# Attention and coupling network on one core: the third rotation and the last norm, state by state or token by token

## What is computed

```python
x = x + layernorm(attention(layernorm(x)))      # 16 heads of 8 features, softmax over 1024 keys
x = x + layernorm(coupling(layernorm(x)))

def coupling(x):                                # _twist([a, b, c, d]) = [c, -d, -a, b], quarters of 64
    gf = global_net(x.mean over tokens)         # one number per sequence
    out = x
    for _ in range(3):
        tf = coupling_net(out)                  # four layers 256-256-128-64-1, one number per token
        k = 0.1 + ar * (0.7 * gf + 0.3 * tf - 0.5) * 2
        out = out + k * _twist(out)
    return out
```

## Time and profile before

| what | us |
|---|---|
| median of 3 runs | 3399.24 (3398.83 to 3399.82) |
| profiled execution: own span | 3391.6 |
| attention stage of a sequence in the middle | 129 |
| coupling stage of a sequence in the middle | 74 |
| from the last exponential to the end | 129 |

### The profile page before, as it was taken

How to read it: one execution, slowest core, us unless ns; L and a number is a source line. 1 busy time by engine, 2 the same in 40 slices (tenths; PEclk the granted TensorE clock), 3 DMA queues, 4 the chain that set the end, 5 groups by cost and what they waited for, 6 DMA issues and landing times.

```text
span 3391.6 us, 56526 instructions
## 1 busy us (share of the span) xinstructions
PE 3222.9 (95%) x19712; PEld 941.5 (28%) x19712; DVE 2992.7 (88%) x5577; ACT 2843.6 (84%) x3752; POOL 897.6 (26%) x1322
## 2 busy tenths in 40 slices
PE   6989999999999999999999999999999999999987
PEld 2222232322323232232322323232232322323223
DVE  7999989999898998989989898998989989898943
ACT  3868979798897979979798897979979798896975
POOL 5002050321505123050320505123050320504015
PEclk7998999999999999999999999999999999999999
DMA  3111111121111112121121111112121121111001
GB/s 90 26 41 43 32 50 33 44 50 44 50 31 51 43 39 55 33 61 32 44 49 44 50 31 51 42 39 55 33 61 32 45 49 44 38 32 51 8 22 38
DMA packets 97498, 144.75 MB, mean 43 GB/s; under 512 B 49472, under 2 KB 60096, under 8 KB 89408
## 3 DMA queue, kind: packets, MB, share of 16 engines
q1 hardware_dynamic: 93520, 123.83, 13.8%
q0 software_dynamic: 3696, 17.31, 2.8%
HBM read 34.61 MB, written 32.51 MB: 20 GB/s over the span
## 4 chain that ended last, share of the span: by engine, by line
PE 67%; DVE 17%; ACT 8%; issue 3%; SPq 2%; DMA 1%; POOL 1%; DVEq 0%; POOLq 0%; ACTq 0%
PE heads_ps L514 24%; PE ring_ps L481 15%; DVE max_parts L966 12%; PE scoresT_ps L499 11%; PE scoresT_ps L602 7%; ACT p_sb L719 4%; DVE stats L977 3%; PE scoresT_ps L607 2%; ACT headsT L728 1%; PE ring_ps L543 1%; SPq L346 1%; DVE state L1030 1%; ACT state L784 1%; DVE moments L987 1%; PE ring_ps L529 1%
## 5 line engine op out<-in xcount | busy, mean ns | idle before, releaser
L966 DVE TENSOR_REDUCE max_parts<-ring_ps 128x1 f32<-128x512 f32 x3744 | 2369.2, 683 | 225.4 <-PE ring_ps L481 166.3
L719 ACT ACTIVATE p_sb<-scoresT_ps 128x1024 f32<-128x1024 f32 x2048 | 1970.1, 1024 | 81.4 <-PE scoresT_ps L499 57.7
L481 PE MATMUL ring_ps<-k_rows,q_rows 48*128 48x512 bf16 x3744 | 1086.0, 384 | 33.1 <-DVE max_parts L966 23.8
L514 PE MATMUL heads_ps<-p_sb,v_sb 128*9 128x512 f32 x8192 | 1071.4, 595 | 17.9 <-ACT headsT L728 11.9
L499 PE MATMUL scoresT_ps<-q_rows,k_rows 51*128 51x512 bf16 x4096 | 1021.3, 383 | 7.1 <-ACT p_sb L719 4.3
L481 PEld LDWEIGHTS ring_ps<-k_rows,q_rows 48*128 48x128 bf16 x3744 | 265.5, 94 | 1353.4 <-DVE max_parts L966 1242.4
L1233 POOL CAST max_wide<-max_all 128x16 bf16<-128x16 f32 x128 | 25.4, 198 | 1743.0 <-DVE max_all L972 1743.0
L602 PE MATMUL scoresT_ps<-state,w 128*128 128x512 f32 x732 | 364.9, 621 | 13.3 <-DVE state L1030 12.3
L824 ACT ACTIVATE p_sb<-scoresT_ps,b 128x512 f32<-128x512 f32 x180 | 123.8, 688 | 194.2 <-PE scoresT_ps L602 193.2
L499 PEld LDWEIGHTS scoresT_ps<-q_rows,k_rows 51*128 51x128 bf16 x4096 | 207.0, 93 | 224.4 <-ACT p_sb L719 211.5
L514 PEld LDWEIGHTS heads_ps<-p_sb,v_sb 128*9 128x9 f32 x8192 | 124.4, 88 | 288.8 <-issue 278.3
(11 more groups left out here) (196 smaller groups left out, 2635.9 us busy)
## 6 DMA issues: line engine op xcount, KB each, us to landing
q_rows<-parts SPq DMA_DIRECT2D x744, 32.0 KB
k_rows<-parts SPq DMA_DIRECT2D x744, 32.0 KB
x_sb<-in_x SPq DMA_DIRECT2D x16, 1024.0 KB, 4.8
x_in<-in_x SPq DMA_DIRECT2D x15, 1024.0 KB, 5.4
out<-x_sb SPq DMA_DIRECT2D x15, 1024.0 KB, 3.9
out<-x_in POOLq DMA_DIRECT2D x15, 1024.0 KB, 7.9
q_rows<-max_rows SPq DMA_DIRECT2D x512, 3.0 KB
feat_h<-headsT SPq DMA_DIRECT2D x512, 16.0 KB
```

What stands on the lines that cost most here:

```text
L481: e.matmul(ring_bank(max_taken, u + 1), q_rows[rows, slot, pair, h * BANK + qb * P:h * BANK + (qb + 1) * P], k_rows[rows, slot, pair, kh * ...
L514: m = e.matmul(heads_ps[32 * j:32 * j + DH + 1, :], v_sb[:, b % 2, kb, 4 * (group % NG) + j, 0:DH + 1], p_sb[:, n % 2, j, :], start=(kb == ...
L719: e.activation(p_sb[:, n % 2, 2 * two:2 * two + 2, :].rearrange("p h n -> p (h n)"), scoresT_ps[:, (2 - 2 * two) * BANK:(4 - 2 * two) * BA ...
L966: e.tensor_reduce(max_parts[:, gi % 2, kh, col:col + 1], bank_of(max_taken, u + 1), AX.X, ALU.max).then_inc(max_taken, 1)
```

## The change

The state is rotated twice only. The third rotation, and the norm behind it, are written as a linear map of the token's row: with coupling numbers k1, k2, k3 of a token, three rotations give `(1 - k1 k2 - (k1+k2) k3) y + (k1 + k2 + (1 - k1 k2) k3) twist(y)`, and the variance of that follows from the moments of the attention's result, which are kept (`keep`). So for each sequence:

- SP copies each rotation's coupling numbers from one partition of `couple` to 128 partitions (`lay_coupling`, six DMAs of 2 KB in pieces of 16 bytes), reloads the attention's result from `out` into `x_in` (`load_back`, beat 12, 1 MB), and stores the finished rows without accumulation (`store_out`, step 32 of the attention); `load_x` moves from the head of an attention to its step 40.
- `take_state` writes the state in another order of tokens: columns `q * 4 + t`, so neighbouring elements of an ACT write stand 16 bytes apart.
- `stats_x` takes two statistics of 128 features in place of one of 256.
- POOL makes `factors` (26 small instructions), `whole_rows` (two of 128x256 for each of eight tiles) and `cross_rows` (four of 128x512) in steps 2 to 16 of the next attention but one, and `keep` at step 18. `make_shift` has one more instruction.
- `turn_back`, `take_back`, `stats_out`, the norm on ACT, its `row_rstd`, `last_half` and the accumulating store go. ACT's tanh (L844) waits for `kappa_laid`, the copy of the rotation before.
- In `ending()` POOL makes `factors`, `whole_rows` and `cross_rows` of sequence 14 in beats 32, 33 and 35, ahead of sequence 15's shift and its first `twist` (beat 36). Behind the beats each half of sequence 15 goes through `factors` on POOL, row products on DVE and ACT side by side, and four crossings on POOL.

```diff
-LAST_BEAT, LAST_STEP = 27, 1
+RELOAD = 12
+LAY_COUPLING = (8, 11)
+FACTORS, WHOLE, CROSS, KEEP = 2, tuple(range(5, 13)), (13, 14, 15, 16), 18
+STORE, LOAD = 32, 40
...
+END_KEEP, END_FACTORS, END_WHOLE, END_CROSS = 24, 32, 33, 35
...
+        def by_token(tile):
+            return tile.rearrange("p (q t) -> p t q", t=TPH)
+
+
+        def other_of(b):
+            return state[:, b % 2, :, :].rearrange("p f (t e) -> p (f t) e", t=TPH)
+
+
+        QUARTER = E // 4
+        CROSSING = ((0, 2, ALU.add), (1, 3, ALU.subtract), (2, 0, ALU.subtract), (3, 1, ALU.add))
+
+        def quarter(tile, first, last, q):
...
+            def load_back(b):
+
+                e.wait_ge(xT_done, 2 * min(b + 4, N))
+                e.wait_ge(mid_stored, 16 * (b + 1))
+                if b:
+                    e.wait_ge(out_stored, 16 * b)
+                e.dma_start(x_in[:, :, :], out_dram[b]).then_inc(x_back, 16)
+
+            def lay_coupling(b, cycle, c):
+                k, before = track(b)
+                if cycle < 2:
+                    e.wait_ge(coupled[k], 4 * before + 2 * cycle + c + 1)
+                else:
+                    e.wait_ge(hid_done[k], end_of(before, cycle, 4, c))
+                if b >= 2 and cycle == 0:
+                    e.wait_ge(scales_ready, b - 1)
+                e.dma_start(kappa[:, b % 2, cycle, TPH * c:TPH * (c + 1)],
+                            couples[k][0:1, c, :]).then_inc(kappa_laid[c], 16)
+
+            def store_out(b):
+                e.wait_ge(out_made, b + 1)
+                e.dma_start(out_dram[b], x_in[:, :, :]).then_inc(out_stored, 16)
...
+                load_back(b - 1)
+                for cycle in range(3):
+                    for c in range(2):
+                        lay_coupling(b - 1, cycle, c)
+                for cycle in range(3):
+                    for c in range(2):
+                        lay_coupling(b, cycle, c)
+                    if cycle == 0:
+                        store_out(b - 1)
...
+                    e.wait_ge(end_added, 4 * (i // 2) + 4)
+                    e.dma_start(out_dram[b][:, rows, :], other_of(b - 1)[:, rows, :]).then_inc(end_stored, 16)
...
+                if valid(b + 2) and 2 <= b + 2 < 4:
                     load_x(b + 2)
+                if valid(b - 2):
+                    lay_coupling(b - 2, 2, 1)
...
+                    if valid(b - 2) and n == STORE:
+                        store_out(b - 2)
+                    if valid(b - 2) and valid(b + 2) and n == LOAD:
+                        load_x(b + 2)
...
+                    if valid(b - 1):
+                        if j == RELOAD:
+                            load_back(b - 1)
+                        for cycle in range(3):
+                            for c in range(2):
+                                if j == CYCLE * cycle + LAY_COUPLING[c]:
+                                    lay_coupling(b - 1, cycle, c)
...
                         e.wait_ge(mean_done, 2 * b)
-                e.activation(state[:, b % 2, f, h * BANK:(h + 1) * BANK], bank_of(state_ready, 4 * b + i + 1), ACT.Copy,
...
                              accum_out=sums[:, f, h:h + 1]).then_inc(state_ready, 1)
-
-            def take_back(b, j):
...
                         e.wait_ge(twist_b_done[k], before)
-                    elif 0 < b < N - 1:
-                        e.wait_ge(last_added, 2 * b - 1 + c)
+                    if b or cycle:
...
-                        take_back(b, i)
+                    e.wait_ge(scales_ready, N + h)
+                    for t in range(h * TPH, (h + 1) * TPH):
+                        m = e.activation(y_sb[:, t, :], x_sb[:, t, :], ACT.Identity, bias=scales[:, 3, t:t + 1],
+                                         scale=scales[:, 1, t:t + 1])
...
                 e.wait_ge(added1, 4 * b + i + 1)
-                row_stats(2, lambda t: x_sb[:, t, :], 2 * i, 2 * i + 2)
+                if b and i == 0:
+                    e.wait_ge(moments_kept, b)
+                for t in range(2 * i, 2 * i + 2):
+                    e.bn_stats(stats[2][:, t, 0:6], x_sb[:, t, :].rearrange("p (q e) -> p q e", q=4)[:, 0:4:3, :])
+                    m = e.bn_stats(stats[2][:, t, 6:12], x_sb[:, t, QUARTER:3 * QUARTER])
...
-                    rows = slice(2 * i, 2 * i + 2)
-                    e.wait_ge(end_rstd, i // 2 + 1)
-                    shift_and_scale(0, lambda t: y_sb[:, t, :], lambda t: y_sb[:, t, :], 2 * i, 2 * i + 2).then_inc(end_norm, 1)
-                    e.wait_ge(end_norm, i + 1)
-                    e.tensor_tensor(y_sb[:, rows, :], y_sb[:, rows, :], x_sb[:, rows, :], ALU.add).then_inc(end_added, 1)
+                    first, last = h * TPH, (h + 1) * TPH
+                    e.wait_ge(scales_ready, N + h)
+                    if h == 0:
...
-            def last_half(b, c):
-
-                cols = slice(c * BANK, (c + 1) * BANK)
-                real, other = state[:, b % 2, 0, cols], state[:, b % 2, 1, cols]
-                e.wait_ge(hid_done[0], end_of(b, 2, 4, c))
-                finished(e.tensor_scalar(couple[:, c, :], couple[:, c, :], ar_token[:, 0:1], shift[0][:, 0:1], ALU.mult,
+                e.tensor_scalar(shift_token[k][:, :], tg[:, :], ar_rest[:, 0:1], 0.1, ALU.mult, ALU.add)
+                finished(e.tensor_scalar(shift[k][:, :], tg[:, :], ar_global[:, 0:1], tenth[:, 0:1], ALU.mult,
                                          ALU.add))
-                if c == 0:
-                    e.wait_ge(state_a_done[0], 4 * b + 4)
-                    e.wait_ge(state_b_done[0], 4 * b + 4)
-                else:
-                    e.wait_ge(last_added, 2 * b + 1)
-                e.tensor_tensor(couple[:, 2, :], couple[:, c, :], other, ALU.mult)
-                finished(e.tensor_tensor(couple[:, 3, :], couple[:, c, :], real, ALU.mult))
-                e.tensor_tensor(real, real, couple[:, 2, :], ALU.add)
-                e.tensor_tensor(other, other, couple[:, 3, :], ALU.subtract).then_inc(last_added, 1)
...
+            def keep(b):
+
+                r, off, cross, spread = (kept[:, b % 2, i, :] for i in range(4))
+                d, d2 = parts_of_mean[:, 0, :], parts_of_mean[:, 1, :]
+                e.wait_ge(rstd_done[2], b + 1)
+                e.tensor_tensor(d, stats[2][:, :, 7], stats[2][:, :, 1], ALU.subtract)
+                e.tensor_tensor(d2, stats[2][:, :, 10], stats[2][:, :, 4], ALU.subtract)
+                e.tensor_tensor(spread, rstd[2][:, :], rstd[2][:, :], ALU.mult)
+                e.tensor_copy(off, offset[2][:, :])
+                finished(e.tensor_copy(r, rstd[2][:, :]))
+                e.tensor_tensor(spread, spread, moments[2][:, :, 1], ALU.mult)
+                finished(e.tensor_tensor(d, d, d2, ALU.add))
+                finished(e.tensor_scalar(d, d, 0.25, None, ALU.mult))
+                finished(e.tensor_tensor(cross, d, r, ALU.mult))
+                e.sem_inc(moments_kept, 1)
+
+            def factors(b, first, last):
+
+                cols = slice(first, last)
+                k1, k2, k3 = (kappa[:, b % 2, i, cols] for i in range(3))
+                r, off, cross, spread = (kept[:, b % 2, i, cols] for i in range(4))
+                f = [factor[:, i, cols] for i in range(6)]
+                whole, turned, whole_off, turned_off = (scales[:, i, cols] for i in range(4))
+                for c in range(first // TPH, last // TPH):
+                    e.wait_ge(kappa_laid[c], 16 * 3 * (b + 1))
+                e.tensor_tensor(f[0], k1, k2, ALU.mult)
+                finished(e.tensor_tensor(f[1], k1, k2, ALU.add))
+                e.tensor_scalar(k3, k3, ar_third[:, 0:1], shift_token[track(b)[0]][:, 0:1], ALU.mult, ALU.add)
+                finished(e.tensor_scalar(f[0], f[0], -1.0, 1.0, ALU.mult, ALU.add))
+                e.tensor_tensor(f[2], f[1], k3, ALU.mult)
+                finished(e.tensor_tensor(f[3], f[0], k3, ALU.mult))
+                e.tensor_tensor(f[0], f[0], f[2], ALU.subtract)
+                finished(e.tensor_tensor(f[1], f[1], f[3], ALU.add))
+                e.tensor_tensor(f[2], f[0], f[0], ALU.mult)
+                e.tensor_tensor(f[3], f[1], f[1], ALU.mult)
+                finished(e.tensor_tensor(f[4], f[1], cross, ALU.mult))
+                e.tensor_tensor(f[5], f[4], f[4], ALU.mult)
+                finished(e.tensor_tensor(f[2], f[2], f[3], ALU.add))
+                finished(e.tensor_tensor(f[2], f[2], spread, ALU.mult))
+                finished(e.tensor_tensor(f[2], f[2], f[5], ALU.subtract))
+                finished(e.tensor_scalar(f[2], f[2], 0.0, EPS, ALU.max, ALU.add))
+                finished(e.tensor_tensor(f[2], f[2], minus_half[:, cols], ALU.pow))
+                e.tensor_tensor(f[0], f[0], f[2], ALU.mult)
+                e.tensor_tensor(f[1], f[1], f[2], ALU.mult)
+                finished(e.tensor_tensor(f[4], f[4], f[2], ALU.mult))
+                e.tensor_tensor(whole, f[0], r, ALU.mult)
+                e.tensor_tensor(turned, f[1], r, ALU.mult)
```

(51 more changed lines are left out.)

167 lines of the change are left out of this document (44 added, 123 removed).

## The result

The changed kernel takes 3463.55 us (median, 3461.62 to 3467.45) against 3399.53 us for the kernel before: 1.0191 times as long, with an interval of 1.0179 to 1.0204. It is slower by 64 us, where 3405.5 us and at most 3426 us had been forecast.

What follows compares the result with a forecast made beforehand. It took ACT and PE to bound attention, and handovers between engines, chiefly DVE to PE before rotation 3, to bound coupling. Span 3391.6 - 12.2 + 18.4 = 3397.8, plus 7.6 around it, 3405.4; forecast 3405.5 us, range 3394 to 3426.

Steps and rivals of the forecast that it cites:

- Faster middle stages: Coupling stages between the first and the ending: removed work less added statistics, a gain of 12.2 us in all.
- "filled" PE's idle time "at no cost": PE's idle ahead of rotation 2 in couplings: the removed transposes had filled it free; 1.11 us idle without them.
- a gain of 18.2 us less 6 for the statistics: Rotation 2 to 3: 1.4 us off each of 13 stages; paired short statistics add 0.4 in each of 15.
- The forecast of 21.4 us for this stretch: Middle couplings: rotation 2 to rotation 3 would take about 21.4 us, a sign that the prediction was right.
- The strided write taken as 0: ACT's `take_state` before the first exponential: writing 16 bytes apart adds 0, with 20 us kept for the range.
- the rival given 0.27: ACT's `take_state`: the strided write is slow, 0.44 us each, 20 us in all, 3425 us; chance 0.27.
- Attention at 0: Attention stages: POOL's added work of about 28 us each hides in its idle time and costs 0.
- The ending, 18.4 forecast: The ending: later rotation 2 of sequence 15 8.8, slower clock 1.6, longer tail 8.0; 18.4 us more.
- the tail: First half's last tanh to the end: copy 3.0, row work 23.2, stores 3.2; 29.4 us, 8.0 more.
- the 2.5 us to be gained early on: Early in the ending: DVE without `stats_out` gains at most 2.7 us, 2.5 after four pairs of statistics.
- cost more than 1.6 us: Ending, after PE idles over 10 us: part of its matmuls run at the lower clock, adding 1.6 us.
- the 7.6 us put around the span: Outside the profiled span: 7.6 us added to the 3397.8 us span, giving 3405.4.

Runs made afterwards that it cites:

- read_turns: `psum_read` with `turn_x`'s transposes made twice at beat 8 and four times at beat 9, sixteen more, all ahead of rotation 2's first layer; 3416.45 us.
- psum_read: The changed kernel with `take_state` reading PSUM by a step of 128 elements and writing the state unbroken, in the same token order; 3428.7 us.
- before_strided: The kernel before with only `take_state` changed to the strided write of the state; 3423.67 us, 1.0072.

## Why the prediction was wrong

*Faster middle stages: the step that failed is that the transposes "filled" PE's idle time "at no cost".* They did, and they kept the granted clock while doing it. Without them PE waits 1.11 us ahead of rotation 2, as in coupling 1 of the kernel before, and in 13 of 14 couplings the first layers then run in part at 1.2 GHz. For rotation 2 to 3, a gain of 18.2 us less 6 for the statistics had been put down, -12.2; it came to +11.7. That is 24 of the 63 us by which the forecast missed the span. The forecast of 21.4 us for this stretch itself was right to 0.1 us wherever the clock stayed: 21.36 in coupling 4, 21.35 in twelve couplings of `read_turns`. Coupling 1 was a sound witness of the queues and a poor one of the clock: it is one stage, and its clock happened to stay. The trace of the kernel before held a warning in coupling 14, as its rotation 3 begins behind a wait of the same kind (granted clock 0.59 in the four us from here):

```profile
3111.59 3.59 PE L602 MATMUL scoresT_ps<-state,w 128*128 128x512 f32 x4 [1.46 <-DVE state L1030]
```

*The strided write taken as 0.* That was the rival given 0.27, with 0.44 us a write and 20 us in all. Measured were 0.48 us a write and 14 to 15 us between rotation 3 and the attentions (14.1 that `psum_read` gives back, 14.9 in `before_strided`; the stretch grew by 17.1 in all). So its place was right and its price near, and the value taken was wrong: it had gone by the nearest row, a copy without a step, against the rule that the prediction itself had cited. The Trainium skill (Advanced Engine Details and Errata, SBUF Cachelines) asks for at least two hits on a line of 16 bytes for full performance. The traces agree, to 0.04 us: 1.08 us with one hit, 0.63 with two, 0.59 with four. Where a row lacks the very thing that a rule speaks of, it is no evidence against the rule.

*Attention at 0.* POOL's block was hidden as worked out: POOL is busy for 26.94 us in attention 8 in place of 12.95, and in `psum_read`, with the same block, all attentions together take as long as before. What was overlooked is that the state's copies reach into the attention: eight attentions begin in part at the lower clock, the sum of all is 14.8 us longer, and `psum_read` gives back all of it. So the longer copies are the cause. By which wait of PE they lose the clock, that for the bank of the maxima or another, is not shown.

*The ending, 18.4 forecast, 23.2 measured.* Three of its terms held: `factors` 7.6 us (3372.31 to 3379.93; 7.5), crossings 5.6 (5.4), the tail 29.6 (29.4). Three were mis-sized. Of the 2.5 us to be gained early on, 0.2 came. ACT's last tanh of sequence 14, then PE's rotation 2 of that sequence, beside the earlier trace rows:

```profile
3369.49 0.69 ACT L885 ACTIVATE couple<-scoresT_ps,b_half 128x512 f32<-128x512 f32 x1 [0.89 <-PE scoresT_ps L673]
...
3349.98 6.71 PE L658 MATMUL scoresT_ps<-state,w 128*128 128x512 f32 x8 [2.99 <-DVE state L1052]
```

Counted from the end of the last exponential (at 3308.13; in the kernel before at 3262.49), rotation 2 begins after 41.9 us in place of 43.3; but its eight products take 6.71 us in place of 5.50, more of them at the lower clock, and the tanh ends after 62.1 us in place of 62.3. So 2.3 us were missing; the copy of the coupling, 2.1 us in place of 3.0, gave 0.9 of them back. POOL's block, 3372.31 to 3397.05, took 24.7 us and not 23.2, for the most part since the products step at 0.66 us and not at 0.6. And the lower clock behind it cost more than 1.6 us: from rotation 2 of the last sequence to the first half's last tanh 30.5 us pass (3400.26 to 3430.77), 27.8 before.

*What else was as predicted.* The short statistics step at 0.2 us. VectorE's timeline in coupling 8, beside the earlier trace rows:

```profile
1916.93 0.28 DVE L1089 BATCH_NORM_STATS2 stats<-x_sb 128x6 f32<-128x128 f32 x1
1917.14 0.27 DVE L1090 BATCH_NORM_STATS2 stats<-x_sb 128x6 f32<-128x128 f32 x1
```

The copies of the coupling land 2.0 us after their issue (median) and hold up nothing in the middle. In the forecast's terms the span is 3397.8 + 24 (rotation 2 to 3) + 17 (rotation 3 to the attention) + 15 (attentions) + 5 (ending) + 2 (all other stretches) = 3461, measured 3460.4. The time missed by 58 us and not by 63 because the 7.6 us put around the span were too many by 5.7: that error hid a part of the others.

*What stays open.* Which waits lose the clock and which do not is not known. Coupling 4 of the changed kernel and couplings 1 and 12 of `psum_read` kept it, behind the same 1.11 us and the same instructions. In the kernels that lost no time at rotation 2 of couplings 1 to 13, one to four of these couplings lost some at rotation 3, and one to four attentions at their start.

## What to carry to other kernels

Work that fills a wait of TensorE may be worth more than its own time: before it is taken out, ask which products follow the wait, and price them at either clock. When a layout needs a step, compare the two sides on which it can stand: here the same order cost 0.48 us a copy on the write and nothing on the read. Work that moves to an idle engine should not stand ahead of the last item's chain, where there is no other item left to cover it.

## What the runs showed of the hardware

- An ACT copy of 128x512 f32 from PSUM into SBUF takes 0.59 us in one piece, 1.08 us with neighbours 16 bytes apart, 0.63 us with pairs of neighbours 16 bytes apart. A read from PSUM by a step of 512 bytes with an unbroken write takes 0.59 us.
- TensorE's granted clock fell to 0.5 (1.2 GHz) behind a wait of 1.1 us in most couplings, not in all. Four products of 128x512 then took 2.6 to 3.7 us in place of 1.95. Sixteen transposes of 0.11 us in the wait kept it at 1.00 at rotation 2 of all 13 couplings that had them; with as many at beats 3 to 6 it fell there in eight of 13.
- VectorE made 16 products and four crossings of one sequence in 8.9 us (3363.06 to 3371.93), where GpSimd took 16.1 (10.5 + 5.6).
